# The delta-rule tail inside the next block, key rows on VectorE, and layernorm centres one step further ahead

## The reference

```python
q = _conv_silu(x @ Wq, conv_q).reshape(b, t, H, DH)
k = _conv_silu(x @ Wk, conv_k).reshape(b, t, H, DH)
v = _conv_silu(x @ Wv, conv_v).reshape(b, t, H, DH)
g_raw = (x @ Wfa @ Wfb).reshape(b, t, H, DH) + dt_bias.reshape(H, DH)
g = -jnp.exp(A_log)[None, None, :, None] * _softplus_stable(g_raw)
beta = jax.nn.sigmoid(x @ Wb)
qf = _l2norm(q) * DH ** (-0.5)
kf = _l2norm(k)

def step(state, inp):
    q_i, k_i, v_i, g_i, b_i = inp
    state = state * jnp.exp(g_i)[..., None]
    inner = jnp.einsum('bhk,bhkv->bhv', k_i, state)
    state = state + jnp.einsum('bhk,bhv->bhkv', b_i[..., None] * k_i, v_i - inner)
    o_i = jnp.einsum('bhk,bhkv->bhv', q_i, state)
    return (state, o_i)
...
g_out = (x @ Wga @ Wgb).reshape(b, t, H, DH)
rstd = jax.lax.rsqrt(jnp.mean(o * o, axis=-1, keepdims=True) + EPS)
o = o * rstd * norm_w * jax.nn.sigmoid(g_out)
return o.reshape(b, t, KD) @ Wo
```

## Time and profile before

| what | us |
|---|---|
| median of 3 runs | 8669.24 (8667.85 to 8671.25) |
| the profiled execution | 8674.82 |
| its span | 8673.0 |
| TensorE busy | 6753.6 (78%) |
| VectorE busy | 3362.8 (39%) |
| ScalarE busy | 2897.8 (33%) |
| GpSimd busy | 2700.0 (31%) |
| delta-rule blocks (first clear to last) | 3392.6 to 6627.1 |

### The profile page before, as it was taken

The page is one execution under the profiler, slowest core; times in us unless marked ns, Lnnn a source line. Parts: engine busy times, 40 slices in busy tenths (PEclk is TensorE's granted clock), DMA queues, the critical chain, the costliest instruction groups (busy, mean ns, idle before and its releaser), DMA issues. The chain is left out here.

```text
span 8673.0 us, 118859 instructions
## 1 busy us (share of the span) xinstructions
PE 6753.6 (78%) x49328; PEld 4649.2 (54%) x49328; DVE 3362.8 (39%) x4762; ACT 2897.8 (33%) x5331; POOL 2700.0 (31%) x1889
## 2 busy tenths in 40 slices
PE   6778776888547886777776777766777999989999
PEld 5566665666335663554544554544454444777444
DVE  3333334333334332444444444444444212545221
ACT  1211121333433333444443443443444112555211
POOL 3344333000000001555555555555554222000222
PEclk7777777888778887888888888888888999989999
DMA  0000000000000000000000000000001111000211
GB/s 20 0 0 0 0 0 24 0 0 0 11 24 0 0 0 13 12 12 12 12 12 17 12 12 12 12 12 16 13 12 57 43 43 30 0 0 0 84 39 47
DMA packets 57522, 132.00 MB, mean 15 GB/s; under 512 B 11126, under 2 KB 21366, under 8 KB 55898
## 3 DMA queue, kind: packets, MB, share of 16 engines
q1 hardware_dynamic: 57178, 126.63, 4.5%
HBM read 124.10 MB, written 2.50 MB: 15 GB/s over the span
## 5 line engine op out<-in xcount | busy, mean ns | idle before, releaser
L568 PE MATMUL ps<-moe_xn_all,moe_w 128*128 128x512 f32 x1792 | 808.2, 594 | 1.7 <-DVE moe_h L681 1.7
L1799 POOL TENSOR_TENSOR kda_rows<-kda_a,kda_f 128x512 f32<-128x512 f32 x225 | 365.1, 1623 | 1260.3 <-DVE kda_a L1780 1101.5
L568 PEld LDWEIGHTS ps<-moe_xn_all,moe_w 128*128 128x128 f32 x1792 | 340.2, 191 | 424.4 <-issue 421.6
L681 DVE TENSOR_TENSOR moe_h<-moe_silu,ps 128x512 f32<-128x512 f32 x224 | 153.9, 687 | 935.7 <-ACT moe_silu L623 928.6
L1751 DVE SCALAR_TENSOR_TENSOR kda_cv<-kda_pre,kda_w_front,kda_cv 128x1024 f32<-128x1024 f32 x297 | 508.1, 1727 | 19.0 <-ACT kda_cv L1693 15.4
L623 ACT ACTIVATE moe_silu<-ps 128x512 f32<-128x512 f32 x224 | 133.7, 597 | 986.0 <-PE ps L568 985.9
L524 POOL TENSOR_TENSOR moe_h<-moe_h,moe_cb 128x512 f32<-128x512 f32 x176 | 233.5, 1327 | 696.5 <-DVE moe_h L681 696.5
L578 PE MATMUL ps<-moe_h,moe_w 128*128 128x512 f32 x896 | 420.3, 592 | 0.0
L1626 PE MATMUL ps<-kda_fa_all,kda_w_front 128*128 128x512 f32 x132 | 129.3, 1111 | 365.4 <-issue 203.6
L1645 PE MATMUL ps<-kda_xn_all,kda_w_front 128*128 128x512 f32 x792 | 368.0, 608 | 48.7 <-ACT kda_gate L1685 44.4
L1799 POOL TENSOR_TENSOR kda_rows<-kda_q,kda_f 128x512 f32<-128x512 f32 x225 | 375.8, 1670 | 0.0
(11 more groups left out here) (483 smaller groups left out, 15799.2 us busy)
## 6 DMA issues: line engine op xcount, KB each, us to landing
kda_w_front<-in_Kw SPq DMA_DIRECT2D x33, 519.0 KB, 4.9
kda_col<-kda_beta SPq DMA_DIRECT2D x33, 512.0 KB, 4.1
moe_w<-in_Mw SPq DMA_DIRECT2D x6, 2816.0 KB, 19.4
moe_cb<-kda_beta SPq DMA_DIRECT2D x64, 256.0 KB, 3.2
moe_cb<-kda_beta SPq DMA_DIRECT2D x32, 224.0 KB, 3.0
moe_cb<-kda_beta SPq DMA_DIRECT2D x32, 192.0 KB, 2.8
moe_cb<-kda_beta SPq DMA_DIRECT2D x32, 160.0 KB, 2.7
moe_w<-in_Mw SPq DMA_DIRECT2D x6, 768.0 KB, 5.7
```

Source lines behind the costliest of these rows:

```text
L568: last = nc.tensor.matmul(ps_gu[u % 2][r], w13[:, k, i, r], n.xn[:, k, cols(c)], start=k == 0, stop=k == KD - 1)
L1799: nc.gpsimd.tensor_tensor(out, halves(src[:], h, 1), halves(o.f[:], h, 1), ALU.mult).then_inc(done, 1)
```

## The change

Four things are changed.

1. `ln_dve`: `centre(0)` and `centre(1)` stand ahead of the loop, `centre(c + 2)` at the start of step c.
2. The tail of block b is taken out of block b and runs in block b + 1, a group at a time between levels (`tail_pe`, `tail_act`, `tail_dve`). All its groups use one PSUM bank (`ps_tail`); its gate product goes through the FRONT banks first of all, its y square sums through them last. After the loop a block of its own runs the last tail. `w_out` has two buffers and is loaded in every block, and the gate's weights are now in it. The block's first tail reads cleared tiles.
3. For levels 1 to 6 VectorE makes the key rows (`a_rows`, `rows_scaled`), GpSimd the query rows and columns; GpSimd's widening of a level waits for VectorE's rows of that level. The widening for level 0 moves from the end of a block to the start of the next.
4. TensorE's `scores(l + 1)` stand behind `t_times_x(l)` and the projection, `copy_x` is one copy of 128x512 where it was two of 128x256, and the front's order is another: project(0) ahead of the decay, both `squares` ahead of `values`; the ScalarE order follows.

Of the lines taken away only some stand below; the functions printed above have them. Lines of the new functions that only collect or return them are left out.

```diff
+    centre(1)
     for c in range(LN_STEPS):
-        if c + 1 < LN_STEPS:
-            centre(c + 1)
+        if c + 2 < LN_STEPS:
+            centre(c + 2)
         root, rstd = n.root[:, c % 2], n.rstd[:, c % 2]
...
+        def tail_pe(pe, o, w, quad):
+            def gate():
+                low_rank(w[:, K_GB - K_WO:K_GB - K_WO + P], ga_all, quad, n.gate_ready)
+            def inner(c):
+                if c == 1:
+                    pe.wait_ge(n.e1_in_sb, 1)
+                for u in range(UNITS):
+                    last = nc.tensor.matmul(ps_tail[:, u], uf[:, c * UNITS + u], o.v[:, 0, u] if c == 0 else e[:, u],
+                                            start=True, stop=True)
+                last.then_inc(n.d_ready, 1)
+            def state():
+                pe.wait_ge(n.d_in_sb, 1)
+                for u in range(UNITS):
+                    last = nc.tensor.matmul(ps_tail[:, u], bg[:, u], d[:, 0, u], start=True, stop=True)
+                last.then_inc(n.z_ready, 1)
+            def y_of(c):
+                if c == 0:
+                    pe.wait_ge(n.z_in_sb, 1)
+                else:
+                    pe.wait_ge(n.d_in_sb, 2)
+                for u in range(UNITS):
+                    if c == 1:
+                        nc.tensor.matmul(ps_tail[:, u], z[:, u], qf[:, u], start=True, stop=False)
+                    last = nc.tensor.matmul(ps_tail[:, u], d[:, c, u], aq[:, c * UNITS + u], start=c == 0, stop=True)
+                last.then_inc(n.y_ready, 1)
+            def right_side():
+                pe.wait_ge(n.gated, 1)
+                for u in range(UNITS):
+                    last = nc.tensor.matmul(ps_tail[:, u], af[:, u], z[:, u], start=True, stop=True)
+                last.then_inc(n.e1_ready, 1)
+            def square_sums(after, count):
+                pe.wait_ge(after, count)
+                pe.wait_ge(n.ysq, 2)
...
+                last.then_inc(n.yss_ready, 1)
+            def out():
+                pe.wait_ge(n.o_ready, 1)
...
+        def tail_act(act):
+            def gate():
+                act.wait_ge(n.gate_ready, 1)
+                nc.scalar.activation(gated[:], two(FRONT), ACT.Sigmoid).then_inc(n.gate_in_sb, 1)
+            def state():
+                act.wait_ge(n.z_ready, 1)
+                nc.scalar.activation(z[:], ps_tail, ACT.Copy).then_inc(n.z_in_sb, 1)
+            def square(c):
+                act.wait_ge(n.y_ready, c + 1)
+                nc.scalar.activation(y_sq[:, :, c * P:(c + 1) * P], ps_tail, ACT.Square).then_inc(n.ysq, 1)
+            def log():
+                act.wait_ge(n.yss_ready, 1)
+                nc.scalar.activation(y_sq[:], two(FRONT), ACT.Ln, scale=1.0 / KDA_HEAD, bias=g.eps[:, 2:3]
+                                     ).then_inc(n.ylog, 1)
+            def root():
+                act.wait_ge(n.ylog, 1)
+                nc.scalar.activation(y_sq[:], y_sq[:], ACT.Exp, scale=-0.5).then_inc(n.yrs, 1)
+        def tail_dve(dve, o, w, quad):
+            def inner(c):
+                dve.wait_ge(n.d_ready, c + 1)
+                nc.vector.tensor_copy(d[:, c], ps_tail).then_inc(n.d_in_sb, 1)
+            def right_side():
+                dve.wait_ge(n.e1_ready, 1)
+                nc.vector.tensor_tensor(e[:], ps_tail, o.v[:, 1], ALU.add).then_inc(n.e1_in_sb, 1)
+            def gate(c):
+                own = slice(c * P, (c + 1) * P)
+                dve.wait_ge(n.gate_in_sb, 1)
+                dve.wait_ge(n.ysq, c + 1)
+                nc.vector.scalar_tensor_tensor(gated[:, :, own], ps_tail, w_vec(w, K_NW - K_WO), gated[:, :, own],
+                                               ALU.mult, ALU.mult).then_inc(n.gated, 1)
+            def scale():
+                dve.wait_ge(n.gated, 2)
+                dve.wait_ge(n.yrs, 1)
+                nc.vector.tensor_tensor(gated[:], gated[:], y_sq[:], ALU.mult).then_inc(n.o_ready, 1)
+            def residual(k):
+                dve.wait_ge(n.out_ready, k + 1)
+                xs = g.x_all[:, k, quad * QUAD:(quad + 1) * QUAD]
+                nc.vector.tensor_tensor(xs, two(OUT[k]), xs, ALU.add).then_inc(n.x_done, 1)
+                if k == KD - 1:
+                    dve.wait_ge(n.x_done, KD)
+        def scale_rows(engine, o, l, r, done):
+            out = rows_s[l % 2][:, r].rearrange("p u (b h) -> p (u b) h", h=h)
+            engine.tensor_tensor(out, halves((o.a, o.q)[r][:], h, 1), halves(o.f[:], h, 1), ALU.mult).then_inc(done, 1)
...
         def chain_pool(pool, cur, nxt):
+            step = Chain(pool, n.g_step)
+            widen(step, cur, 0)
             for l in range(1, LEVELS):
+                h = 1 << l
+                scale_rows(nc.gpsimd, cur, l, 1, n.scaled)
+                nc.gpsimd.tensor_tensor(halves(cols_s[l % 2][:], h, 0), halves(cur.col[:], h, 0),
+                                        halves(decay_g[:], h, 0), ALU.mult).then_inc(n.scaled, 1)
+                pool.wait_ge(n.scaled, 2 * l)
+                pool.wait_ge(n.rows_scaled, l)
+                widen(step, cur, l)
+            nc.gpsimd.tensor_tensor(colg, cur.col[:, :, 0:P], decay_g[:, :, 0:P], ALU.mult).then_inc(n.final_scaled, 1)
+            pool.wait_ge(n.y_ready, 2)
+            first_rows(pool, nxt)
...
+            tail.gate()
...
             scores(0)
+            f.project(0)
+            lt_times_t(0)
+            tail.inner(0)
+            f.decay()
             scores(1)
+            tail.state()
             for l in range(1, B_LEVELS):
+                lt_times_t(l)
+                if l == 1:
+                    tail.y_of(0)
+                elif l == 2:
+                    tail.right_side()
+                elif l == 3:
+                    tail.inner(1)
+                t_times_x(l, 0)
+                t_times_x(l, 1)
+                if l < 3:
+                    f.project(l)
+                elif l == 3:
+                    tail.y_of(1)
+                elif l == 4:
+                    f.squares(0)
                 if l < B_LEVELS - 1:
                     scores(l + 1)
                 else:
                     last_scores()
+            last_x()
+            f.squares(1)
+            last_dt()
+            f.values()
+            pe.wait_ge(n.final_scaled, 1)
+            pe.wait_ge(n.gated, 2)
+            tail.square_sums(m.vt_in_sb, 1)
+            tail.out()
...
+            tail.gate()
+            f.project(0)
             f.decay()
+            tail.state()
             f.exp_decay()
+            f.one_plus()
+            copy_x(1)
+            tail.square(0)
+            f.project(1)
+            f.log_decay()
+            copy_x(2)
+            f.inverse()
+            f.silu(0)
+            f.project(2)
+            copy_x(3)
+            f.square(0)
+            tail.square(1)
+            copy_x(4)
+            f.silu(1)
+            f.square(1)
+            copy_x(5)
             f.silu(2)
+            f.log_sum(0)
+            copy_x(B_LEVELS, upper)
+            f.log_sum(1)
+            act.wait_ge(n.e1_in_sb, 1)
+            f.values()
+            act.wait_ge(n.t_ready, 2 * B_LEVELS + 1)
+            tail.log()
+            f.decays()
+            f.root(0)
+            f.root(1)
+            tail.root()
+            nc.scalar.activation(bg[:], ps_tail, ACT.Copy).then_inc(n.bg_in_sb, 1)
...
+            def a_rows(l):
+                dve.wait_ge(n.g_step, 2 * l)
+                if l >= 2:
+                    dve.wait_ge(n.sc_ready, l - 1)
+                scale_rows(nc.vector, o, l, 0, n.rows_scaled)
...
+            a_rows(1)
+            dve.wait_ge(n.lt_ready, 1)
+            nc.vector.tensor_tensor(t[:, :, 1], lt[:, 0], ident, ALU.add).then_inc(n.t_ready, 1)
+            dve.wait_ge(n.x_ready, 1)
+            nc.vector.tensor_tensor(t[:, :, 0], ps_x, ident, ALU.add).then_inc(n.t_ready, 2)
+            tail.inner(0)
             f.clip()
+            f.tap(0, 0)
             masks(1)
+            dve.wait_ge(n.t_ready, 3)
+            update(1)
+            a_rows(2)
+            f.tap(0, 1)
+            tail.gate(0)
+            masks(2)
+            f.tap(0, 2)
+            update(2)
+            tail.right_side()
+            a_rows(3)
+            f.tap(1, 0)
+            masks(3)
+            f.tap(1, 1)
+            update(3)
+            tail.inner(1)
+            a_rows(4)
             f.corr(0)
+            masks(4)
+            f.tap(1, 2)
+            update(4)
+            tail.gate(1)
+            a_rows(5)
             f.corr(1)
+            f.tap(2, 0)
+            masks(5)
+            f.tap(2, 1)
+            update(5)
+            a_rows(6)
+            f.tap(2, 2)
+            last_masks()
             f.corr(2)
             f.q_row()
             f.a_row()
             f.column()
+            tail.scale()
+            tail.residual(0)
+            tail.residual(1)
...
-                todo = [lt, aq_b, aq, uf, *cols_s, *pre]
+                todo = [lt, aq_b, aq, uf, bg, final_rows, w_out[0], ops[1].v, *cols_s, *pre]
...
```

(20 more changed lines are left out.)

488 lines of the change are left out of this document (181 added, 307 removed).

## The result

The changed kernel takes 8735.88 us (8733.41 to 8737.47, four runs) where the kernel before takes 8670.24 (8667.85 to 8675.89): a ratio of 1.0075, 95% interval 1.0057 to 1.0092. It is slower by 66 us, as forecast (8740). The profiled execution took 8735.65 us, its span is 8733.6 and its mean granted clock 0.853, so it is told against the span of 8673.0.

The account below looks back on a forecast made before the run. No engine is full; the delta-rule layer is bound by a chain of handovers. Blocks +74, extra tail block +36, clears +1 and layernorms −40 give +71 on 8674.8, so 8745.8, as a median 8740; range 8620 to 8830.

Parts of the forecast that it names:

- layernorms −40: All eight layernorms: centring one step further ahead shortens the steps, −40 us in all.
- the extra tail block +36: After the loop: one more tail block, run once, adds 36 us.
- blocks +74: The 32 delta-rule blocks: each +2.3 us, +74 in all.
- head: Block start to level 1's first matmul: from 14.85 to 17.1 us, +2.3.
- Levels 1 to 3: Levels 1 to 3 of a block: from 22.8 to 29.65 us, +6.85, with scores, masks, tail groups and table loads.
- Levels 4 and 5: Levels 4 and 5: stall behind three taps goes, level 4 −4.35 us, level 5 −1.35.
- Closing part and gap: Block end after the last updates: from 35.2 to 33.4 us, −1.8; the gap to the next block left alone.
- Each level also carries a group of the tail (about 1.0): Levels 1 to 3: a tail group at each level adds about 1.0 us.
- It buys about nothing: Rows moved to VectorE: relieving GpSimd, not what ends last at levels 1 to 5, gains about nothing.
- 1.2 us a row: Key rows on VectorE, six of 128x512 a block: 1.2 us each, between bounds 0.69 and 1.77.
- Rival (d): Moved rows: GpSimd and VectorE take turns, 2.3 us a row instead of 1.2, +5.6 a block, 8845; chance 0.07.
- Rival (a): Blocks: handovers close better, TensorE avoids half clock, scores hidden; −1.5 to −3 us a block, 8618 to 8570; chance 0.22.

Follow-up runs that it names:

- scores_early: The changed kernel with the scores of level l + 1 ahead of the second product of level l, VectorE's order turned the same way: 8559.2 us.
- copies_first: The changed kernel with ScalarE's copy of x at levels 1 and 2 ahead of the exponential and logarithm with their table loads: 8738.7 us.
- tail_quarter: The changed kernel with TensorE doing the tail's groups for one sequence of four, every wait kept: 8718.3 us.
- all_four: The changed kernel with y_root_first, scores_early, copies_first and one_table together: 8238.2 us.
- y_root_first: The changed kernel with ScalarE's y root right behind the y logarithm and VectorE's scaling ahead of q, a and column: 8567.1 us.
- rows_on_pool: The changed kernel with the key rows of levels 1 to 6 back on GpSimd: 8763.7 us.
- one_table: The changed kernel with one function table holding both exponential and logarithm, so four table loads a block remain of seven: 8722.2 us.
- both orders: The changed kernel with y_root_first and scores_early together: 8309.9 us.

## Why the prediction was right

**Time and sign.** 8740 forecast, 8735.9 measured. Its large terms stand: layernorms −40 (−37 by a run of its own), the extra tail block +36 (37.1 in the trace), blocks +74 (67.5). Two hits are in part luck. The items that I wrote down for the tail block sum to 26.5, and with a copy of about 0.7 for each group to 30, not 36. And the clears came out 103.4 apart, as forecast, only because the first distance grew by 11 us, as the clear now lies 16 us later in its block; the other 31 grew by 2.06, not 2.3. The preamble was put at +1 and gave 3.1 − 7.6 = −4.5: without the gate and with the decay behind the first projection the first front is shorter by more than the share that I had set against the clears.

**The stretches were less exact than their sum.** In the odd block: head 14.85 to 15.4, where 17.1 was forecast: with 3.01 us of idle ahead the gate ran at full clock (1.95 for 3.75), as in 14 of 16 odd blocks; even blocks have 3.78, behind 6.6 us of idle or more. Levels 1 to 3: +7.8 against +6.85. Levels 4 and 5, to the last update: −6.0 against −5.7; the stall went as forecast, and what is late next is in part VectorE: corr(1) and the tap stand ahead of the masks of level 5, 2.40 us of idle. Closing part and gap: +0.1 against −1.8, by the out projection at 6.24 for the 5.2 I took and the scaling at 2.40 for 1.2. So the stretches miss by −1.7, +1.0, −0.3 and +1.9, which add to +0.9 only: that they offset each other is luck. In the mean of 30 blocks the four stretches change by +0.3, +7.7, −6.0 and −0.1.

**Why levels 1 to 3 grew** was half right. Scores and masks behind the projection are half of it: scores_early takes 3.8 of the 7.7 us off levels 1 to 3 (and 2.2 off levels 4 and 5). The table loads ahead of the x copy do make TensorE wait, as written: copies_first takes 2.2 us off levels 1 and 2, though the edits gave 0 to 14 us in all. "Each level also carries a group of the tail (about 1.0)" in the open is wrong for this kernel: by tail_quarter the groups at levels 1 and 2 lie in that same wait. With the waits gone they seem to come into the open: in all_four levels 1 and 2 take 8.9 each where the kernel before has 7.8, about one group of 1.16 more; no run takes the group out there.

**The closing part** was right and undervalued: I wrote down the decays, both roots, and VectorE's q, a and column with the scaling as 8.3 us on the path, and left it at that. y_root_first confirms 5.3 of them.

**The rows.** "It buys about nothing" is wrong, the move buys 28 us. "It is not what ends last at levels 1 to 5" was right: by rows_on_pool GpSimd isn't late even with the key rows. It then runs beside VectorE's clip and tap in the head, which take longer, and TensorE is granted a lower clock; those two are what the traces show behind the 28 us. My 1.2 us a row is wrong by almost two, 0.68. "GpSimd loses 9 us" is wrong too: over 31 blocks it is busy 2.6 us a block less than before (1707 to 1628), since what is left to it takes longer. Its widening of g has a mean of 1.92 us, and 1.24 in rows_on_pool and in the kernel before. Rival (d), that the moved rows pay, didn't come: they have a median of 0.682 us and a maximum of 1.325, because GpSimd mostly stands waiting for them. That wait and the longer widening stand in one row of the page (busy, mean ns, idle before):

```profile
L1915 POOL TENSOR_TENSOR kda_g<-kda_g,kda_f 128x512 f32<-128x512 f32 x224 | 430.3, 1921 | 1089.1 <-DVE kda_rows L1907 842.2
```

The rule of the Trainium skill ("SBUF — State Buffer", "Who interferes with whom") isn't refuted by the short rows; the trace agrees with it elsewhere: the scaling beside GpSimd's rows took 2.40, and 1.23 away from them.

**Rival (a)** named the clock as a way to end faster. A part of it came: squares(0) ran at full clock (1.98 for 3.46) and the first product of level 4 too (1.15 for 1.77 in the mean). Squares(1) and the out projection, behind 2.64 and 10.79 of idle, stayed slow, as I had held against it. The clock is also what couples the block's terms: two orders that give 346 us apart give 426 together, copies and table give 11 or 72 (the layernorms, outside the blocks, do add). The sum on record didn't have that; TensorE's busy time over 31 blocks was 2203 before and 2193 after, so for this change it happened not to matter.

## What to carry to other kernels

Work moved off a closing chain is worth only as much as what stands behind it: look at the order of the short operations that are left (here four on ScalarE and four on VectorE, 169 us), and put next to the critical chain what it waits for, the rest behind. On TensorE let independent products cover the wait for a copy, not the time behind it (177 us, with VectorE's order turned to match). An engine that isn't late can still cost by what it runs beside: the tap took 2.28 for 1.28 when GpSimd had the key rows. When taking a wait away changes nothing, compare TensorE's busy time and granted clock for the same matmuls before dropping the edit: copies_first and one_table looked worthless alone and gave 72 us on the kernel with both orders.

## What the hardware showed that I had not expected

The granted clock of TensorE fell in one stretch after an edit that took waits away in another: over 31 blocks copies_first has 2.1 us less idle a block, and the busy time of the same matmuls is 71 us higher. Thirteen products without use a block made the kernel 160 us faster. Which idle brings the fall on isn't settled: the clock was full behind 3.01 us of idle (the gate, odd block) and half behind 2.64 (squares(1)), so the wait just ahead doesn't decide alone. The gate itself shows it best: in odd blocks it stands behind 3.01 us of idle (once 3.30), with the key rows on VectorE or on GpSimd, and runs at full clock in 14 of 16 blocks of the changed kernel and in 5 of 16 of rows_on_pool. What went on in the stretch ahead of it differs, and no run here varied that by itself. Nor was the tail's interleaving tried without its new orders; that both beats the kernel before by 360 us (37 of them from the layernorms) says that interleaving, rows and orders together gain 10 us a block (323/32), not how the gain divides.
